# W2's magnitude sums in the weight products, its ternary blocks made on VectorE in tiles 0 to 2 and kept in DRAM

## The chip, the cores and the metric

One Trainium2 chip, all 8 NeuronCores. Each core takes one of the 8 sequences (2048 tokens of 1024 features) and runs the same program alone; nothing is exchanged. The metric is the device time of the slowest core in microseconds. PE is TensorE, ACT is ScalarE, DVE is VectorE, POOL is GpSimd, and SP only issues transfers and waits for what they need; its queue is taken in program order, so a transfer that waits holds back the ones behind it.

## The reference, cut to what matters

Two layers. Layer 0 adds a decayed causal attention and an int4-quantised projection with a low-rank term. Layer 1 adds a chunked linear recurrence (here a masked scores product per tile of tokens) and an FFN whose weights are rounded to -1, 0, 1:

```python
def _quantize(W):
    gamma = jnp.mean(jnp.abs(W))
    return jnp.clip(jnp.round(W / (gamma + EPS)), -1.0, 1.0)
Wq1 = _quantize(W1)                        # W1 is 4096 x 1024
Wq2 = _quantize(W2)                        # W2 is 1024 x 4096
h = jax.nn.relu(jnp.einsum('bsd,fd->bsf', x, Wq1) + b1)
out = jnp.einsum('bsf,df->bsd', h, Wq2) + b2
```

So each matrix (16 MB in f32) is read twice: once for the mean of its magnitudes, once to compare it with plus and minus half of gamma.

## The kernel before, in words

Every engine's program is one list in program order; `do` appends an instruction with the tokens it waits for, and a token is a semaphore count. There is no scheduler: the order of the Python calls is the order on each engine. PSUM is eight banks of 128x512 f32, taken in turn (`take`), and `freed[b]` is the eviction that a bank's next user waits for.

The stages in order: the product Wvo, the first norm and layer 0's V for 16 chunks of 128 tokens; then two weight products of 16 groups of 8 matmuls each, **Wp** (L484 to L493, W_read by W_write) and **G** (L496 to L506, Wq by Wk), each group evicted by ACT. `kern`, the int4 matrix, is loaded behind Wp (L519) and rounded by DVE. Then four tiles of 512 tokens (`j`). Each tile runs `scores0(j)` (P blocks, masked and evicted by DVE), `out0(c)` for its four chunks (P by V and x by Wf, then residual, norm and a transposing DMA), `gproj(j+1)` (8 groups, ACT evicts), `vproj` of four chunks (8 groups, ACT evicts), `scores1(j)` (4j+4 groups, DVE evicts to P) and `pv1(c)` (P by V, DVE adds). The FFN follows: per tile 32 groups `ffn1(j, fc)` with a Relu on ACT, and two `pair(c)` calls, each a Strassen product of 2x2 blocks: seven products of 16 matmuls from differences of h (`diff`, DVE, L1010) and sums of W2 blocks (`w2_sum`, DVE, L981).

The FFN's weights are made beside the tiles. `stat_unit` (L581) sums one 128x1024 block's magnitudes on ACT: 32 blocks of W1, then 32 of W2, each loaded by SP four units ahead, from tile 0's `out0` to tile 2's. `thr_sums` and `thr_scale` turn the sums into thresholds. `w1_begin` and `w1_end` (L810, L815) make a ternary W1 block on DVE in two instructions, in tiles 2 and 3. W2 is made in tile 3 and during `ffn1(0)`: `w2_begin` (L827) takes two signs on ACT, `w2_end` (L835) adds them on DVE, which gives 0 and plus or minus 2, and the Relu has the scale 0.5 for it. `w2_sums` mixes the 20 block sums in between.

SBUF limits when things can be made: W2's ternary blocks lie in R0 and R1, free only after `out0(15)` and `gproj(3)`; W1's in R5 and R2, and R2 holds Wf until `out0(15)`.

Of the kernel before, what the change touches and what calls it, by code (L numbers as in the profile page):

```python
# [14 lines left out]
D = 1024  # L15
# [74 lines left out]
def build_nc():  # L90
# [27 lines left out]
    res_d = nc.dram_tensor("res_d", [T, D], F32, kind="Internal").ap()  # L118
    bnc = nc.dram_tensor("bnc", [1, 16], F32, kind="Internal").ap()
# [156 lines left out]
    ch_yt = [chan(f"yt{k}") for k in range(6)]  # L276
# [206 lines left out]

    Wp = XR.ap().bitcast(BF16)  # L484
    wp_tok = [None] * 16
    for dc in range(8):
        for hf in range(2):
            b = take()
            t_wm = group(b, [(R[3][:, k * 1024 + dc * 128:k * 1024 + (dc + 1) * 128],
                              R[4][:, k * 1024 + hf * 512:k * 1024 + hf * 512 + 512],  # L490
                              t_ww[k // 4], t_wr[k // 4]) for k in range(8)])
            wp_tok[2 * dc + hf] = ev_act_scale(
                Wp[:, dc * 1024 + hf * 512:dc * 1024 + hf * 512 + 512], b, alp, t_wm, t_al, *nrm[12:])  # L493

# [4 lines left out]
    for dc in range(8):  # L499
        for hf in range(2):  # L500
# [5 lines left out]
                G[:, dc * 1024 + hf * 512:dc * 1024 + hf * 512 + 512], b, 1.0 / 32.0, t_gm)  # L506


    kqf = [Rf[3][:, 0:2048], Rf[3][:, 2048:4096], Rf[4][:, 0:2048], Rf[4][:, 2048:4096]]
    ch_kn = [chan(f"kn{k}") for k in range(4)]  # L510
# [6 lines left out]
    t_kn = []  # L517
    for k in range(4):
        t_kn.append(ch_kn[k].dma(sp, kqf[k], rows(kern, 2 * k, 2), t_wm))  # L519
# [45 lines left out]

    ch_st = [chan(f"st{k}") for k in range(4)]
    st_used = [None] * 4
    st_n = [0]
    st_land = [None] * 64

    def stat_load(u):
        k = u % 4
        if u < 32:
            dc, q = divmod(u, 4)
            src = bass.AP(W1T.tensor, 128 * dc * DFF + q * 1024, [[DFF, 128], [1, 1024]])
        else:
            src = rows(W2T, u - 32)
        fr = st_used[k] if u >= 4 else wf_tok[15]
        st_land[u] = ch_st[k].dma(sp, st_slot[k], src, fr)

    def stat_unit(n=1):  # L581

        for _ in range(n):
            u = st_n[0]
            if u >= 64:
                return
            st_n[0] += 1
            k = u % 4
            st_used[k] = act.do(lambda s, k=k, u=u: s.activation(  # L589
                st_slot[k], st_slot[k], AF.Abs, accum_out=wsum[:, u:u + 1]), st_land[u], t_ldb[2])  # L590
            if u + 4 < 64:
                stat_load(u + 4)

    t_thr = [None]
    ch_bt = chan("bt")

    def thr_sums():
        dve.quiet(lambda v: v.reduce_sum(gs[:, 0:1], wsum[:, 0:32], axis=AX.X), st_used[3])
        tb = dve.do(lambda v: v.reduce_sum(gs[:, 1:2], wsum[:, 32:64], axis=AX.X))
        t1 = pool.do(lambda g: g.tensor_reduce(gsr[0:1, :], gs, axis=AX.C, op=ALU.add), tb)  # L600
        t1 = ch_bt.dma(sp, bnc[0:1, 2:4], gsr[0:1, :], t1)
        t_thr[0] = ch_bt.dma(sp, gsr, bass.AP(bnc.tensor, 2, [[0, 128], [1, 2]]), t1)

    def thr_scale():
        t1 = pool.do(lambda g: g.tensor_scalar(gsr, gsr, 1.0 / (DFF * D), EPS_BN, ALU.mult, ALU.add), t_thr[0])
        pool.quiet(lambda g: g.tensor_scalar(thr, gsr, 0.5, None, ALU.mult), t1)
        t_thr[0] = pool.do(lambda g: g.tensor_scalar(nthr, gsr, -0.5, None, ALU.mult))

# [23 lines left out]
    def scores0(j):  # L632
        for i in range(4 * j, NCH):
# [9 lines left out]
                P[:, i * 512:i * 512 + w], pb[b][:, 0:w], mask[m][:, 0:w], ALU.mult), tok, mk_tok[n])  # L643
# [84 lines left out]
    def pv1(c):  # L728
# [11 lines left out]
        ch, q = (ch_ys, pool) if c < 8 else (ch_yt, sp)  # L740
        y_tok[c] = ch[c % 6].dma(q, bass.AP(res_d.tensor, c * 128 * D, [[D, 128], [1, D]]), buf, t)


    xrs = [XR[:, 1024 * k:1024 * k + 1024] for k in range(4)]
    stage = st_slot + xrs + [MC[:, :], b2r[:, :]]
    ch_g = [chan(f"g{k}") for k in range(10)]
    stage_free = [None] * 10

    order = [0, 1, 2, 3] * 8 + [4, 5, 6, 7] * 4 + [9, 8, 0, 1] * 4
    w2_order = [h + 4 * q + i for q in range(4) for h in (0, 16) for i in range(4)]  # L750
    w1_tok = [None] * 4
    w2_tok = [None] * NF
    q_user = [None] * 10
    q_done = {}
    q_tok = {}
# [9 lines left out]
    def unit_load(u):  # L765

        s = order[u]
        if stage_free[s] is None or (q_user[s] is not None and q_user[s] not in q_done):
            return False
        if u < 32:  # L770
            fb, dc = divmod(u, 8)
            src = bass.AP(W1T.tensor, 128 * dc * DFF + fb * 1024, [[DFF, 128], [1, 1024]])
        else:
            src = rows(W2T, w2_order[u - 32])
        q_tok[u] = ch_g[s].dma(sp, stage[s], src, *stage_free[s])
        q_user[s] = u
        return True

    def unit_done(u, t):
        q_done[u] = t  # L780
        stage_free[order[u]] = (t,)

    class Units:


        def __init__(self, lo, hi, begin, end):
            self.ld, self.nx, self.hi = lo, lo, hi
# [415 lines left out]
```

## Time and profile before

| | |
|---|---|
| time, median of 3 runs | 1036.56 us (1035.12 to 1140.85) |
| profiled execution | 1036.97 us, span 1035.4 us |
| spans of the eight cores | 1025.7 to 1035.4 us |
| mean granted TensorE clock of the cores | 0.983 to 0.993 |
| busy: PE, DVE, ACT, POOL | 978.0, 486.0, 382.2, 107.8 us |
| DMA | 133.9 MB, mean 129 GB/s |

A row of a timeline has the start, how long the group lasted from its first start to its last end, the engine, the line, the operation with its tiles and shapes, the count, and in brackets the idle time before it and who ended it. PE's rows can lack a few matmul records. In a table of stretches the columns are the stretch, the busy time of PE, weight loads, DVE, ACT and POOL with the number of instructions, then the granted clock, the DMA engines' share and their rate.

### The profile page before, as it was taken

What the parts mean: (1) busy time and instruction counts of PE and PEld (TensorE: products, weight loads), DVE (VectorE), ACT (ScalarE), POOL (GpSimd) and SP (SyncE); (2) the same over time, 40 slices, a digit from 0 to 9 for tenths busy, and PEclk for the clock granted to TensorE, in tenths of its full rate; (3) what the DMA queues carried; (4) which work ended last, traced back from release to release, by engine and by line L of the source; (5) the groups of instructions that cost most, each with busy time, mean ns of one, the idle gap of its engine ahead of it and who ended that gap; (6) DMA issues with size and microseconds to landing.
All of it is one profiled execution on the core that took longest, in us unless ns stands there. A gap on an engine that the chain in (4) does not pass through costs nothing.

```text
span 1035.4 us, 12956 instructions; the slowest of 8 cores (1025.7 to 1035.4 us)
## 1 busy us (share of the span) xinstructions
PE 978.0 (94%) x4579; PEld 447.4 (43%) x4656; DVE 486.0 (47%) x658; ACT 382.2 (37%) x609; POOL 107.8 (10%) x93
## 2 busy tenths in 40 slices
PE   4899999999999999999896988989999999999998
PEld 1445444444444454445342333434444444444443
DVE  0587025633145144568687789693007300730073
ACT  0566433425865744310125686600330033003300
POOL 3200000045014301600320000000000000000000
PEclk9999999999999999999999899999999999999999
DMA  9999551079897982547358775102100210020001
GB/s 137 198 232 226 94 162 47 1 215 207 244 304 216 259 262 92 124 141 231 104 149 257 240 254 198 41 31 92 41 1 31 91 41 1 31 92 1 1 31 51
DMA packets 58544, 133.91 MB, mean 129 GB/s; under 512 B 21458, under 2 KB 21842, under 8 KB 58482
## 3 DMA queue, kind: packets, MB, share of 16 engines
q1 hardware_dynamic: 48082, 107.76, 34.5%
q0 software_dynamic: 10112, 25.24, 11.6%
q8 instruction: 38, 0.62, 0.2%
q14 instruction: 24, 0.20, 0.1%
q10 hardware_dynamic: 288, 0.10, 0.0%
HBM read 124.75 MB, written 16.78 MB: 137 GB/s over the span
## 4 chain that ended last, share of the span: by engine, by line
PE 80%; DMA 7%; DVE 6%; issue 4%; ACT 2%; POOL 1%; SPq 0%; DVEq 0%; ACTq 0%; POOLq 0%
PE pb L232 69%; PE pb L683 10%; DMA XR<-W2T 2%; DMA R<-WoT 2%; DVE R L989 1%; DVE R L837 1%; DMA b2r<-W2T 1%; DVE R L818 1%; DMA R<-W1T 1%; POOL R L81 1%; PE pb L310 1%; ACT xnat L830 1%; DVE P L721 1%; PE pb L542 0%; DVE xnat L299 0%
## 5 line engine op out<-in xcount | busy, mean ns | idle before, releaser
L232 PE MATMUL pb<-XN,R 128*128 128x512 bf16 x1251 | 278.5, 382 | 11.9 <-ACT V L947 10.3
L232 PEld LDWEIGHTS pb<-XN,R 128*128 128x128 fp8e4 (+1 forms) x1280 | 125.6, 98 | 164.3 <-issue 15.9
L947 ACT ACTIVATE V<-pb,smallS 128x512 bf16<-128x512 f32 x128 | 85.5, 685 | 251.4 <-PE pb L232 251.4
L232 PE MATMUL pb<-R,XN 128*128 128x512 bf16 (+3 forms) x561 | 117.6, 361 | 1.2 <-ACT R L348 0.4
L232 PE MATMUL pb<-R,P 128*128 128x512 fp8e4 x512 | 113.7, 383 | 5.1 <-DVE P L1017 5.1
L1017 DVE TENSOR_TENSOR P<-V 128x2048 bf16<-128x2048 bf16 x32 | 38.1, 1218 | 166.0 <-ACT V L947 166.0
L1046 DVE TENSOR_TENSOR R<-pb,R 128x512 f32<-128x512 f32 x80 | 52.6, 686 | 78.4 <-PE pb L232 78.3
L232 PEld LDWEIGHTS pb<-R,P 128*128 128x128 bf16 x512 | 50.4, 99 | 67.2 <-issue 8.3
L232 PEld LDWEIGHTS pb<-R,XN 128*128 128x128 bf16 x576 | 53.8, 98 | 57.8 <-issue 4.0
L589 ACT ACTIVATE R<-R 128x1024 f32<-128x1024 f32 x64 | 67.1, 1050 | 13.7 <-DMA R<-W1T 8.3
L232 PE MATMUL pb<-R 128*128 128x512 bf16 x314 | 69.2, 379 | 1.1 <-ACT R L343 0.8
L683 PE MATMUL pb<-V,P 128*128 128x512 bf16 x268 | 64.3, 380 | 4.8 <-DVE P L642 4.5
L232 PE MATMUL pb<-V,P 128*128 128x512 bf16 x265 | 61.3, 389 | 7.0 <-DVE P L721 5.3
L232 PE MATMUL pb<-XN 128*128 128x512 bf16 (+3 forms) x316 | 61.3, 353 | 5.1 <-DVE P L721 4.9
L683 PE MATMUL pb<-R,XN 128*128 128x512 bf16 x251 | 61.3, 385 | 0.2
L232 PE MATMUL pb<-XR,V 128*128 128x512 fp8e4 x256 | 56.6, 379 | 0.0
L232 PE MATMUL pb<-XR,XN 128*128 128x512 bf16 x250 | 55.7, 379 | 0.7 <-DMA XN<-xnat 0.4
L232 PEld LDWEIGHTS pb<-R 128*128 128x128 bf16 x320 | 31.2, 98 | 38.5 <-issue 1.2
L702 POOL TENSOR_TENSOR R<-R,b2r 128x1024 f32<-128x1024 f32 x16 | 37.9, 2371 | 92.2 <-ACT R L701 90.1
L232 PEld LDWEIGHTS pb<-XN 128*128 128x128 bf16 x320 | 30.7, 99 | 36.4 <-issue 7.8
L348 ACT CAST V<-pb 128x512 bf16<-128x512 f32 x64 | 35.9, 589 | 25.3 <-PE pb L232 24.9
L691 DVE TENSOR_TENSOR R<-pb,R 128x512 f32<-128x512 f32 x32 | 21.5, 686 | 49.0 <-PE pb L683 37.3
(112 smaller groups left out, 901.9 us busy)
## 6 DMA issues: line engine op xcount, KB each, us to landing
R<-W1T SPq DMA_DIRECT2D x64, 512.0 KB, 6.0
R<-W2T SPq DMA_DIRECT2D x40, 512.0 KB, 5.9
XR<-x SPq DMA_DIRECT2D x16, 512.0 KB, 8.8
R<-x POOLq DMA_DIRECT2D x16, 512.0 KB, 10.4
XR<-W2T SPq DMA_DIRECT2D x16, 512.0 KB, 5.8
R<-res_d SPq DMA_DIRECT2D x16, 512.0 KB, 4.0
out<-R SPq DMA_DIRECT2D x32, 256.0 KB, 2.0
R<-kern SPq DMA_DIRECT2D x4, 1024.0 KB, 12.2
```

The lines of the kernel that those rows point to most:

```text
L81: q.prog.append((after, lambda e: e.dma_start(dst, src, **kw), self.sem, 16))
L232: t.matmul(o, lhs, rhs, start=f, stop=l))
L310: fn = (lambda p, dc=dc: p.transpose(pbB[b][:, dc * 128:(dc + 1) * 128], o[:, dc * 128:(dc + 1) * 128], ident[:, :]))
L348: t = act.do(lambda s: s.copy(o, pb[b][:, 0:n]), tok, *after)
L589: st_used[k] = act.do(lambda s, k=k, u=u: s.activation(st_slot[k], st_slot[k], AF.Abs, accum_out=wsum[:, u:u + 1]), st_land[u], t_ldb[2])
L683: t.matmul(pb[bs[hf]][:, :], lhs, rhs, start=f, stop=l))
L691: t = dve.do(lambda v, hf=hf: v.tensor_tensor(buf[:, hf * 512:hf * 512 + 512], pb[bs[hf]][:, :], buf[:, hf * 512:hf * 512 + 512], ALU.add) ...
L702: b2_tok[c] = pool.do(lambda g: g.tensor_add(buf, buf, b2r[:, :]), tr, t_b2)
L721: t = dve.do(lambda v, b=b, a=a, k=k: v.scalar_tensor_tensor(P[:, a:a + 512], pb[b][:, :], rx[:, -k - 1:-k], CV, ALU.mult, ALU.mult), tok, ...
L947: t = act.do(lambda s: s.activation(hid(fc), pb[b][:, :], AF.Relu, scale=0.5, bias=b1h[:, fc:fc + 1]), tok, t_b1h)
L1017: d_tok[k] = dve.do(lambda v: v.tensor_tensor(dst, Hv[:, x[0], x[1]], Hv[:, y[0], y[1]], ALU.subtract), h_tok[15] if k == "6" else h_tok[3 ...
L1046: done[blk] = dve.do(lambda v, blk=blk, op=op: v.tensor_tensor(r[blk], r[blk] if op == ALU.subtract else pb[b][:, :], pb[b][:, :] if op == ...
```

## The change

1. `stat_unit`'s order is turned round: W2's 32 blocks first, then W1's. Twenty of W2's sums now run during the weight products, six behind the last six groups of Wp and fourteen behind the first fourteen of G, with the P tile as four staging buffers. The other twelve run in `gproj(0)` and `scores0(0)`, W1's thirty-two in tiles 0 to 2, with two staging buffers each.
2. W2's threshold is ready in tile 0. `w2_unit` makes one ternary block by the two DVE instructions that W1 had (`low` and `high`), over the block just read, and SP stores its 128 KB to the DRAM tensor `w2q_d`. Two buffers take turns: the load of a block waits for the store of the one two before it. The 32 units are spread over tiles 0 to 2.
3. In tile 3 `w2_fetch` reads the blocks back: 2 MB and 1 MB before `vproj`, the last 1 MB (into the place of two staging buffers) after the last W1 unit.
4. The 20 sums stand together at the start of `ffn1(0)`. The ACT signs are gone, the Relu has no scale.
5. The stores of chunks 8 to 15 to `res_d` go through POOL's queue, as those of 0 to 7 did. kern's load is issued before G's sums; the small tables come after them.

```diff
+    def stat_place(n):
+        if n < 20:
+            return n % 4, n - 4
+        if n < 32:
+            return 6 + n % 2, n - 2 if n >= 22 else -1
+        return 4 + n % 2, n - 2 if n >= 34 else -1
...
+    for n in range(4):
+        stat_load(n, lgt[15], t_k[1])
     Wp = XR.ap().bitcast(BF16)
...
                 Wp[:, dc * 1024 + hf * 512:dc * 1024 + hf * 512 + 512], b, alp, t_wm, t_al, *nrm[12:])
+            if dc >= 5:
+                stat_unit()
+    for k in range(4):
+        t_kn.append(ch_kn[k].dma(sp, kqf[k], rows(kern, 2 * k, 2), t_wm))
...
                 G[:, dc * 1024 + hf * 512:dc * 1024 + hf * 512 + 512], b, 1.0 / 32.0, t_gm)
+            if dc < 7:
+                stat_unit()
+    for n in range(20, 22):
+        stat_load(n, t_gm)
...
+    def low(a, src, e, tok):
+        return dve.do(lambda v: v.tensor_scalar(
+            A8s[a], src, nthr[:, e:e + 1], None, ALU.is_lt, saturate=False), tok, a_free[a], t_thr[e])
+    def high(a, dst, src, e, tok, *after):
+        a_free[a] = dve.do(lambda v: v.scalar_tensor_tensor(
+            dst, src, thr[:, e:e + 1], A8s[a], ALU.is_gt, ALU.subtract, saturate=False), tok, *after)
+    def w2_load(u):
+        k = u % 2
+        w2_land[u] = ch_w2[k].dma(sp, st_slot[2 + k], rows(W2T, u), w2_kept[u - 2] if u > 1 else st_tok[30 + k])
+    def w2_unit():
...
+        if 0 < u < NF - 1:
+            w2_load(u + 1)
+        src = st_slot[2 + k]
+        dst = src.bitcast(FP8)[:, 0:1024]
+        t = high(k, dst, src, 1, low(k, src, 1, w2_land[u]))
+        w2_kept[u] = ch_w2s[k].dma(sp, w2q_d[:, u * 1024:u * 1024 + 1024], dst, t)
...
     for ec, t_g in gproj(0):
-        pass
+        if ec % 2 == 1:
+            stat_unit()
...
+        if j == 3:
+            w2_fetch(0, 16, t_o0[15], xb_tok[15])
+            w2_fetch(16, 8, t_o0[15])
         for m in range(4):
             t_v1 = vproj(4 * j + m, Wp, wp_tok)
-            stat_unit()
+            if j < 2:
+                if m != 2:
+                    w2_unit()
+                if m % 2 == 1 or j == 1 and m == 0:
+                    stat_unit()
...
             if j == 3:
-                w1u.step(2, t_o0[15])
+                w1_unit(1 + m % 2, t_o0[15])
...
+    w2_fetch(24, 8, w1_done[30], w1_done[31])
...
-            if j == 0 and fc in (0, 2, 4, 6, 9, 11, 13, 15, 18, 20, 22):
-                w2u.step(1)
-                w2_sums(2)
+                for q in range(4):
+                    for n in ("12+22", "21+11", "11-22"):
+                        w2_sum(n, q, t_v1, w1_done[31])
+                    for n in ("11+12", "21+22"):
+                        w2_sum(n, q, s_tok["12+22", q], s_tok["21+11", q])
```

**SP's queue around the weight products.** The rows are SP's transfers in program order, target<-source with the shape; R<-kern is the int4 matrix, MC and A the mask tables. Before:

```order
L81 DMA XR<-x 128x1024 x12
L81 DMA b2r<-b 128x1024
L81 DMA MC<-tabF 128x512 x2
L81 DMA A<-negT 128x512
L81 DMA R<-kern 128x2x1024 x4
L81 DMA R<-tabF 128x1024
L81 DMA R<-negT 128x512
L81 DMA R<-b 128x1024
```

Now:

```order
L81 DMA XR<-x 128x1024 x12
L81 DMA P<-W2T 128x1024 x10
L81 DMA R<-kern 128x2x1024 x4
L81 DMA P<-W2T 128x1024 x10
L81 DMA R<-W2T 128x1024 x2
L81 DMA b2r<-b 128x1024
L81 DMA MC<-tabF 128x512 x2
L81 DMA A<-negT 128x512
L81 DMA R<-tabF 128x1024
L81 DMA R<-negT 128x512
L81 DMA R<-b 128x1024
```

Ten block loads stand ahead of kern and ten behind it, and the tables come last.

**DVE in tile 0, from the end of `out0(3)` to `pv1`.** xnat is the normalised chunk, the evictions to P are `scores1(0)`'s. Before:

```order
L299 TENSOR_SCALAR xnat<-R,col 128x1024
L718 TENSOR_TENSOR P<-pb,MC 128x512
L718 TENSOR_TENSOR P<-pb,MC 128x384
L718 TENSOR_TENSOR P<-pb,MC 128x256
L718 TENSOR_TENSOR P<-pb,MC 128x128
L736 TENSOR_TENSOR R<-pb,R 128x512 x8
```

Now (the two rows of a unit, `low` and `high`, stand seven times in turn where the dots are; two of them are shown):

```order
L299 TENSOR_SCALAR xnat<-R,col 128x1024
L791 TENSOR_SCALAR A<-R,col 128x1024
L795 SCALAR_TENSOR_TENSOR R<-R,col,A 128x1024
L791 TENSOR_SCALAR A8b<-R,col 128x1024
L795 SCALAR_TENSOR_TENSOR R<-R,col,A8b 128x1024
...
L745 TENSOR_TENSOR P<-pb,MC 128x512
L745 TENSOR_TENSOR P<-pb,MC 128x384
L745 TENSOR_TENSOR P<-pb,MC 128x256
L745 TENSOR_TENSOR P<-pb,MC 128x128
L763 TENSOR_TENSOR R<-pb,R 128x512 x6
```

DVE had nothing between the norm and the first P eviction; seven units are there now.

## Rows read from the trace of the kernel before

**Rows 1.** Busy time by stretches; columns as told above.

```profile
560.00:600.00 40.00, 32.85 (x148) 14.64 (x150) 30.97 (x37) 28.72 (x27) 0.00 (x0) 0.91 0.77 254
```

**Rows 2.** PE's timeline from tile 3's scores1 to the first pair.

```profile
530.26 20.88 PE L232 MATMUL pb<-XN 128*128 128x512 bf16 x94
555.70 5.75 PE L232 MATMUL pb<-XN 128*128 128x512 bf16 x24 [4.56 <-DVE P L721]
...
614.91 13.60 PE L232 MATMUL pb<-XN,R 128*128 128x512 bf16 x55 [4.09 <-ACT V L947]
...
665.76 7.07 PE L232 MATMUL pb<-XR,V 128*128 128x512 fp8e4 x32
...
684.98 8.75 PE L232 MATMUL pb<-R,P 128*128 128x512 fp8e4 x32 [4.01 <-DVE P L1017]
```

**Rows 3.** ACT's timeline: evictions of G, gproj(0)'s last, then magnitude sums in tile 0.

```profile
140.95 0.60 ACT L343 ACTIVATE R<-pb 128x512 bf16<-128x512 f32 x1 [1.04 <-PE pb L232]
...
165.13 0.60 ACT L343 ACTIVATE R<-pb 128x512 bf16<-128x512 f32 x1 [1.13 <-PE pb L232]
...
180.66 0.58 ACT L348 CAST R<-pb 128x512 bf16<-128x512 f32 x1 [0.27 <-PE pb L232]
...
229.83 1.04 ACT L589 ACTIVATE R<-R 128x1024 f32<-128x1024 f32 x1
...
230.87 1.04 ACT L589 ACTIVATE R<-R 128x1024 f32<-128x1024 f32 x1
...
259.59 1.06 ACT L589 ACTIVATE R<-R 128x1024 f32<-128x1024 f32 x1
...
261.58 1.07 ACT L589 ACTIVATE R<-R 128x1024 f32<-128x1024 f32 x1
```

**Rows 4.** DVE's groups by shape: busy us, mean ns of one, idle before.

```profile
L989 DVE TENSOR_TENSOR R<-R 128x2048 fp8e4<-128x2048 fp8e4 x12 | 26.8, 2284 | 0.1
...
L818 DVE SCALAR_TENSOR_TENSOR R<-R,col,A 128x1024 fp8e4<-128x1024 f32 x16 | 20.4, 1277 | 0.0
...
L721 DVE SCALAR_TENSOR_TENSOR P<-pb,col,MC 128x512 bf16<-128x512 f32 x24 | 17.7, 746 | 33.7 <-PE pb L232 33.7
...
L812 DVE TENSOR_SCALAR A<-R,col 128x1024 fp8e4<-128x1024 f32 x16 | 12.0, 747 | 10.7 <-DMA R<-W1T 10.3
```

**Rows 5.** The chain of waits: start, us, what; tile 3 and ffn1(0).

```profile
523.52 3.04 DMA XN<-xnat
...
617.45 11.34 DMA b2r<-W2T
```

**Rows 6.** Busy time by stretches of 8 us.

```profile
120.00:128.00 8.00, 7.95 (x38) 3.64 (x38) 0.00 (x0) 3.44 (x5) 0.00 (x0) 1.00 0.00 0
...
620.00:628.00 8.00, 7.95 (x38) 3.64 (x38) 8.00 (x5) 4.96 (x7) 0.00 (x0) 1.00 0.99 371
```

**Rows 7.** Timeline: kern's issues on SP, DVE's first and last reduction of it.

```profile
139.21 3.24 SPq L81 DMA_DIRECT2D R<-kern  x4
...
146.23 2.29 DVE L524 TENSOR_REDUCE col<-R 128x1 f32<-128x2048 f32 x1 [31.06 <-DMA R<-kern]
...
156.29 2.29 DVE L524 TENSOR_REDUCE col<-R 128x1 f32<-128x2048 f32 x1 [0.26 <-DMA R<-kern]
```

**Rows 8.** PE's timeline: gproj(0), gproj(1), and pv1(0)'s start.

```profile
166.59 13.98 PE L232 MATMUL pb<-XN,R 128*128 128x512 bf16 x63
...
250.25 13.76 PE L232 MATMUL pb<-XN,R 128*128 128x512 bf16 x62
...
282.22 4.26 PE L232 MATMUL pb<-V,P 128*128 128x512 bf16 x19
```

**Rows 9.** The answer on the tensor W2T, time to landing.

```profile
DMA to landing us min/median/max: 3.3/5.9/12.1
```

**Rows 10.** The page's DMA issues: KB each, median us to landing.

```profile
out<-R SPq DMA_DIRECT2D x32, 256.0 KB, 2.0
...
res_d<-R SPq DMA_DIRECT2D x8, 512.0 KB, 5.5
```

## What I expect of it

> **What bounds it.** I read the cores and the granted clock first, then TensorE's (PE's) busy time in stretches, its own timeline where it pauses, and last the engines it waits for. All cores are within 1%, and the profiled execution lasted 1036.97 us (span 1035.4), 0.04% over the median, so the sum is made against it. PE is the bound nearly everywhere; in 560 to 600 it is busy 32.9 of 40 us at a mean granted clock of 0.91 [rows 1]. The pauses lie between the start of tile 3's scores1 (530.26) and the fifth product of the first pair (684.98): 4.56 us behind a P eviction, 4.09 behind a Relu, 4.01 behind a diff [rows 2]. The work there is 116 matmuls of scores1 (12 groups of 8, and 20 for the narrow four), 116 of pv1 (2 x (13+14+15+16)), 256 of ffn1, 64 of four products: 552. A group of 8 takes 1.727 us ((165.13 - 140.95)/14 [rows 3]), so the work is 119.2 us; 154.7 pass. **35.5 us are waits and low clock.** What ends them is the making of W2: two signs on ScalarE, an add on DVE, and the sums between, all queued ahead of evictions.
>
> **Term 1, W2's work leaves tile 3: -34.2.** The signs, the adds and their loads go. What stays on DVE during ffn1(0) is 20 sums of 2.28 us [rows 4], 45.7 us. They begin some 4 us into ffn1 (the last W1 unit and two evictions stand before them) and end by 50, under ffn1's 55.3; the third stretch of sums needs the last 1 MB fetch, some 5 us, and is 22 us away. So diffs no longer queue behind sums. The low clock behind the last pause goes too: 32 matmuls took 8.75 us after it and 7.07 before it [rows 2]: 1.7 us. A new wait stays. SP now fetches 3.15 MB of ternary W2 right after the last transposition (523.52 [rows 5]); at 371 GB/s [rows 6] that is 8.5 us, and W1's fifth load queues behind it to about 536. DVE then closes six units before the first scores1 eviction, at about 541; before, it had eight units there. Per pair of groups it needs two evictions and a unit, about 2 x 0.75 + 0.75 + 1.28 = 3.5 us [rows 4] against PE's 3.45, so the lag stays until the last narrow groups, and pv1(12), which begins after 25 us (555), waits for its P block until about 558: +3. Sum: -35.5 - 1.7 + 3 = -34.2. Bounds: +0 (the lag is caught up) and +9 (the loads come 6 us later).
>
> **Term 2, W2's magnitude sums move into the weight products: +14.7.** ScalarE can do it: two evictions and a sum start to start are 1.99 us, a sum alone 1.04 [rows 3], so eviction plus sum is 1.52 against 1.727. The DMA can't. From 120, a few groups into Wp, the queues are empty [rows 6], the first four loads land well before their use at 131, but the next ones start only as sums free their slots. The sixth sum ends at about 141.1 (Wp's last eviction, 139.2, plus 0.69 and 1.04, some queueing), and in SP's order kern's four 1 MB loads come next (issued in 3.24 us [rows 7]), then again ten stat loads. The kern loads land one after the other, 3.15 MB from 146.23 to 156.29, 313 GB/s [rows 7], and a small load behind six others took 11.34 us [rows 5]: the queue is served in order. With 1 MB of stat loads ahead and a start 2 us later the last kern load lands 3.4 us later, at 159.7, and the eleventh stat load behind it at 161.4. That sum is due at 148.9: ScalarE waits 12 us, and every eviction of G behind it. Eight banks hold PE for 13.8 us; the real price comes at the end. The next nine loads land 1.67 us apart (0.52 MB at 313 GB/s), the twentieth sum starts at 176.4, and the fifteenth eviction of G, which every group of gproj(0) needs, ends at 176.4 + 1.04 + 0.5 = 178. It ended at 165.7 [rows 3], and the first group, begun at 166.6 [rows 8], reached its last matmul 1.5 us later, at 168.1. **+10.** The tables for masks, half of which were loaded long before, now stand behind stat loads 20 to 22 (3.3 us) and are 1.8 MB (5.9 us): the masks, ahead of gproj's evictions on ScalarE, come at about 187, as much later as PE. But three more sums stand between gproj's evictions and the last of them, which scores0 waits for as it did at 180.66 [rows 3]: 3 x 1.04, **+3**. A pause of 8 us or more costs the low clock after it, 1.7 as above. Bounds for all of term 2: +3 if the bytes interleave well (12.6 MB from 131 at 371 GB/s end at 165, and then ScalarE's own 1.52 us pace decides), +18 if the tables bring a second pause of 4 us with its clock.
>
> The Trainium skill, page "HBM Reference", section "Specifications (TRN2)", gives a core about 358 GB/s when both of a pair stream. By that, kern would take 11.7 us instead of 13.4 and each load 1.46, term 2 would be near +11, and the whole 1015. A stretch of this trace shows 371, the kern loads 313; the sum keeps 313, for it is the same transfer at the same place.
>
> **Term 3, 32 W2 units on DVE in tiles 0 to 2: +1.** Each is 0.75 + 1.28 us, 65 us in all; DVE was idle over half of the time there, and the ten in out0 sit between chains that PE doesn't wait for. The tight place is a block of seven units from the end of out0(3) to scores1(0), twice (tile 1 has it too). Each of two slots goes load, unit, store, and the next load waits for the store to land: three such cycles, less one store, stand between the issue of the load for the block's third unit (8 us after gproj begins at 250.25 [rows 8]) and the seventh unit's end. A W2T load took 3.3 at least and 5.9 in the middle with four in flight [rows 9]; a 256 KB store 2.0 [rows 10]. I take 4.5 + 1.95 + 2.0 = 8.45, for at most two loads are in flight, and a 128 KB store is nearest to the 256 KB one. The seventh unit ends at 8 + 25.4 - 2 = 31.4, scores1 ends at 32 (282.22 - 250.25), and there pv1 wants its first P, which an eviction after that unit makes: half a microsecond each. Bounds: 0 with 3.3, and 4.5 per block with 5.9, plus its clock.
>
> Small edits at nothing: the bias halving (one 128x32 instruction), the Relu's scale (same instruction), the stores of res_d in tiles 2 and 3 that go from SP's queue to POOL's (POOL has nothing else due, and the reload is wanted only 55 us later). If POOL's store became late, res_load would be, and the pair's first gather with it. The waits at 484 to 526 stay; W1's loads there are the same.
>
> **Sum: 1036.97 - 34.2 + 14.7 + 1 = 1018.5, taken as 1018.** A measurement of this kernel tells about 2% from no change, that is below 1016 or above 1057.
>
> **Rivals.**
> *The weight stage swallows the sums.* If the loads get through between kern's, ScalarE's pace decides: term 2 is +3, the clock stays, the rest as above: 1036.97 - 34.2 + 3 + 1 = 1007. For it: the DMA is idle from 120, and 371 GB/s has been moved. Against: kern's landings one behind the other, and the eleventh load's place behind them. 0.24.
> *The blocks of units are late.* With the 5.9 us load each block ends 4.2 us later: 2 x (4.2 + 1.7) = 12, less the 1: 1029. For: the median load. Against: it belongs to four in flight. 0.17.
> *Slower than before: the round trip through DRAM.* The next load waits for the store of ternary bytes. If a load takes 5.9 and the store 5.5, as the res_d stores of SP did [rows 10], the cycle is 13.35 instead of 8.45, three of them 14.7, less 3.5 for the longer last store: 11.2 us per block, two blocks 22, two more units in tile 1's scores1 5, clock 3.4: 1018 + 30 = 1048. Against: a quarter of the bytes, and an emptier queue. It turns a gain into a loss once the cycle is above 11 us. 0.09. The Trainium skill, "DMA: Bandwidth & Descriptors", section "Anatomy of one DMA — SWDGE (gpsimd) path", told of GpSimd's path, warns of a surprisingly long delay when a completed write has HBM as its target, which speaks for this rival; the 2.0 us stores of out in this trace speak against it.
>
> **Numbers.** The forecast has 0.46, with its own range 1011 to 1026; the three rivals 0.24, 0.17 and 0.09, and 0.04 is for what I don't see. Eight in ten reaches from the quick case with term 1 at its best (1004) to the late blocks with their bounds: 1003 to 1034. Faster by over 2%: the quick case, and of the forecast's own range the third below 1016: 0.24 + 0.15 + 0.01 = 0.40. Slower by over 2% needs the DRAM cycle at its worst or something unseen: 0.05. Within: 0.55.
>
> **What would show it.** ScalarE's timeline between 140 and 180: one wait of about 12 us for a W2T load, and PE idle some 10 us before gproj(0) (right); no such wait (the quick rival). DVE's first scores1 eviction in tiles 0 and 1 within a microsecond of PE's, or several behind. In tile 3 no pause over 4 us, ffn1(0) in 55 us from first to last group, and the sums done before it ends. If PE still pauses in ffn1(0), term 1 is wrong; if pv1(12) waits for much more than 3 us, the fetch is the cause.

## The result and the profile after

The changed kernel takes **1063.51 us** (median of 4 runs, 1061.57 to 1065.93) against 1036.56 for the kernel before, run beside it: ratio **1.0258** (1.0223 to 1.0294), slower. Forecast were 1018 us and a range that ended at 1034. Executions in which one die ran at a lower clock (1140.85 us, say, for the kernel before) are left out of every ratio; two of e9_early_late's four were such, so it has none and stands again, unchanged, as e12_early_late.

Where it goes is read first from the starts of the program's stages on PE. Each number below is the start of a stage's first matmul, as the median over the eight cores of a kernel's profiled execution, minus the same of the kernel before. The three columns are the three terms of the prediction: term 2 is the shift at gproj(1), term 3 what comes on top until tile 3's scores1, term 1 what comes after, until ffn1(1) starts (behind all that tile 3's W2 work had delayed). The last column is the time against the kernel before on the same chip, with its 95% interval; less than 2% either way counts as the same time.

| kernel | term 2 (to gproj(1)) | term 3 (to scores1(3)) | term 1 (to ffn1(1)) | ratio |
|---|---|---|---|---|
| predicted | +14.7 | +1 | -34.2 | 0.982 |
| changed kernel | +18.2 | **+34.9** | -27.7 | 1.0258 |
| e1_a8 | +20.4 | +28.3 | -26.8 | 1.0250 (1.0233-1.0267) |
| e2_weights | +21.6 | +33.7 | -27.3 | 1.0262 (1.0238-1.0286) |
| e3_fetch_late | +21.4 | +35.5 | **-35.7** | 1.0184 (1.0139-1.0229) |
| e4_all | +22.0 | +27.4 | -35.7 | 1.0132 (1.0112-1.0151) |
| e5_noload | +16.8 | **+3.2** | -25.7 | 0.9917 (0.9903-0.9932) |
| e6_nogloads | +11.3 | +32.9 | -28.5 | 1.0170 (1.0150-1.0190) |
| e7_early | +17.2 | **+8.5** | -27.8 | 1.0011 (0.9993-1.0028) |
| e8_aside | +19.4 | +20.8 | -27.8 | 1.0187 (1.0159-1.0215) |
| e9_early_late | +19.3 | +9.0 | -35.2 | (as e12) |
| e10_room | **+0.3** | +44.5 | -35.6 | 1.0086 (1.0054-1.0119) |
| e11_spread | +1.2 | +35.4 | -35.9 | 1.0047 (1.0028-1.0065) |
| e12_early_late | +18.9 | +10.1 | -35.7 | **0.9942 (0.9920-0.9964)** |
| e13_trip | +0.4 | +29.5 | -35.6 | 0.9992 (0.9965-1.0018) |
| e14_now1sums | +0.6 | +13.9 | -35.5 | 0.9774 (0.9759-0.9790) |
| e15_last | +0.3 | +32.4 | -35.8 | 0.9988 (0.9972-1.0004) |

The lines below are the changed kernel's slowest core (span 1061.0). **Tile 3**, PE's timeline (start, us, instruction, in brackets the idle time before it and what ended it), which answers [rows 2]:

```profile
583.92 13.98 PE L233 MATMUL pb<-XN 128*128 128x512 bf16 x64
600.00 11.41 PE L233 MATMUL pb<-XN 128*128 128x512 bf16 x64 [2.10 <-DVE P L748]
612.70 2.32 PE L233 MATMUL pb<-V,P 128*128 128x512 bf16 x10 [1.29 <-DVE P L748]
...
618.99 24.29 PE L233 MATMUL pb<-V,P 128*128 128x512 bf16 x104 [2.08 <-DVE P L745]
643.12 55.42 PE L233 MATMUL pb<-XN,R 128*128 128x512 bf16 x256
698.37 7.07 PE L233 MATMUL pb<-XR,V 128*128 128x512 fp8e4 x32
705.27 13.98 PE L233 MATMUL pb<-R,P 128*128 128x512 fp8e4 x64
```

All 256 matmuls of ffn1(0) are one line of 55.42 us and the products follow at full pace: the pauses of before are gone. From scores1(3) to ffn1(0) 59.2 us pass for 50.1 of work, so new waits of 9 us are left; DVE's and SP's timelines name the cause:

```profile
592.43 0.75 DVE L791 TENSOR_SCALAR A8b<-R,col 128x1024 fp8e4<-128x1024 f32 x1 [7.48 <-DMA R<-W1T]
```
```profile
578.56 0.95 SPq L81 DMA_DIRECT2D R<-w2q_d  x2
579.60 32.69 SPq L81 DMA_DIRECT2D R<-W1T  x10
```

W1's next load stands behind the 3 MB fetch, and DVE's evictions stand behind the block that waits for it.

**Weight stage and tile 0**, first ScalarE's timeline, then DVE's, then two lines of DVE's before (answers to [rows 3, 7]):

```profile
161.88 1.06 ACT L519 ACTIVATE P<-P 128x1024 f32<-128x1024 f32 x1 [13.16 <-DMA P<-W2T]
...
191.71 0.81 ACT L653 ACTIVATE R<-R 128x128 f32<-128x128 f32 x2 [11.88 <-DVE R L650]
```
```profile
150.94 2.29 DVE L594 TENSOR_REDUCE col<-R 128x1 f32<-128x2048 f32 x1 [35.50 <-DMA R<-kern]
...
160.32 2.29 DVE L594 TENSOR_REDUCE col<-R 128x1 f32<-128x2048 f32 x1 [0.46 <-DMA R<-kern]
162.72 0.16 DVE L596 TENSOR_REDUCE col<-col 128x1 f32<-128x4 f32 x1
174.79 0.15 DVE L601 TENSOR_SCALAR col<-col 128x1 f32<-128x1 f32 x1 [11.92 <-DMA col<-bnc]
...
191.26 0.75 DVE L650 SCALAR_TENSOR_TENSOR R<-R,col 128x128 f32<-128x128 f32 x2 [5.49 <-DMA R<-negT]
```
```profile
164.85 0.15 DVE L531 TENSOR_SCALAR col<-col 128x1 f32<-128x1 f32 x1 [6.01 <-DMA col<-bnc]
...
175.75 0.74 DVE L624 SCALAR_TENSOR_TENSOR R<-R,col 128x128 f32<-128x128 f32 x2
```

Kern's last block is 4.0 us later than before (160.32 against 156.29); forecast was 3.4. Behind it stands a chain: the maximum goes through DRAM to all partitions (11.92 us between; before 6.01), the quantisation, and the first mask, which now waits 5.49 us for its table. 4.0 + 5.9 + 5.5 = 15.4: the first mask comes at 191.26 where it came at 175.75. ScalarE's exponential of it (191.71, after a wait of 11.88) stands in front of gproj(0)'s evictions, and PE has eight banks. But PE's own gproj(0), held by G's evictions behind the wait of 13.16, ends only at 193.85: in this kernel the two paths end together.

**The units.** DVE's timeline in tile 0's scores1 block, then SP's at its start:

```profile
281.30 0.75 DVE L791 TENSOR_SCALAR A8b<-R,col 128x1024 fp8e4<-128x1024 f32 x1 [3.58 <-DMA R<-W2T]
282.16 1.29 DVE L795 SCALAR_TENSOR_TENSOR R<-R,col,A8b 128x1024 fp8e4<-128x1024 f32 x1
285.58 0.75 DVE L791 TENSOR_SCALAR A<-R,col 128x1024 fp8e4<-128x1024 f32 x1 [2.14 <-DMA R<-W2T]
...
290.90 0.75 DVE L791 TENSOR_SCALAR A8b<-R,col 128x1024 fp8e4<-128x1024 f32 x1 [3.18 <-DMA R<-W2T]
...
295.93 0.75 DVE L791 TENSOR_SCALAR A<-R,col 128x1024 fp8e4<-128x1024 f32 x1 [2.88 <-DMA R<-W2T]
...
300.40 0.75 DVE L791 TENSOR_SCALAR A8b<-R,col 128x1024 fp8e4<-128x1024 f32 x1 [2.33 <-DMA R<-W2T]
...
304.48 0.75 DVE L791 TENSOR_SCALAR A<-R,col 128x1024 fp8e4<-128x1024 f32 x1 [1.94 <-DMA R<-W2T]
...
306.54 1.68 DVE L745 TENSOR_TENSOR P<-pb,MC 128x512 bf16<-128x512 f32 x4
```
```profile
283.52 0.33 SPq L81 DMA_DIRECT2D w2q_d<-R  x1
283.94 0.39 SPq L81 DMA_DIRECT2D R<-W1T  x1
286.08 0.33 SPq L81 DMA_DIRECT2D R<-W2T  x1
```

Every unit waits for its load, and scores1(0)'s evictions, on whose P pv1 waits, come last. A slot comes round after 9.6 us here (281.30, 290.90, 300.40); the forecast had 8.45. In tile 1 a slot takes 13 to 17 us, and behind the units stand the products with the masks:

```profile
327.69 0.75 DVE L791 TENSOR_SCALAR A8b<-R,col 128x1024 fp8e4<-128x1024 f32 x1 [4.12 <-DMA R<-W2T]
...
335.85 0.75 DVE L791 TENSOR_SCALAR A<-R,col 128x1024 fp8e4<-128x1024 f32 x1 [3.62 <-DMA R<-W2T]
```

Between 306 and 345 a W2T load takes 6.9 us in the middle and a 128 KB store 4.5, with x's loads (9.9) and res_d's stores (8.7) among them. Over the program such a store takes 1.7 to 8.6 us, 3.6 in the middle; I had put 2.0.

### The profile page after: what moved, and what is told of

Same layout as the page of the kernel before. It is cut to its first block, busy times and chain, and to the rows that moved or that the text cites. A ratio compares the mean times of both kernels' runs of the same rounds, so it can differ in the third digit from the quotient of the medians.

```text
span 1061.0 us, 13017 instructions; the slowest of 8 cores (1046.2 to 1061.0 us)
## 1 busy us (share of the span) xinstructions
PE 989.5 (93%) x4656; PEld 449.3 (42%) x4656; DVE 512.5 (48%) x689; ACT 313.7 (30%) x545; POOL 118.3 (11%) x105
## 3 DMA queue, kind: packets, MB, share of 16 engines
q1 hardware_dynamic: 52116, 111.95, 34.2%
## 4 chain that ended last, share of the span: by engine, by line
PE 66%; DMA 20%; DVE 7%; issue 3%; ACT 1%; SPq 1%; POOL 1%; DVEq 0%; ACTq 0%; POOLq 0%
PE pb L233 56%; PE pb L710 10%; DMA R<-W2T 6%; DMA w2q_d<-R 4%; DMA P<-W2T 2%; DVE R L795 2%; DMA XR<-x 2%; DMA R<-WoT 2%; DMA R<-negT 1%; DMA R<-W1T 1%; DVE A L791 1%; DMA P<-Wd 1%; DVE xnat L299 1%; SPq L81 1%; ACT P L519 1%
## 5 line engine op out<-in xcount | busy, mean ns | idle before, releaser
L969 ACT ACTIVATE V<-pb,smallS 128x512 bf16<-128x512 f32 x128 | 88.0, 687 | 337.4 <-PE pb L233 337.4
L233 PE MATMUL pb<-R,XN 128*128 128x512 bf16 (+3 forms) x576 | 120.9, 365 | 5.8 <-ACT R L348 5.8
L1068 DVE TENSOR_TENSOR R<-pb,R 128x512 f32<-128x512 f32 x80 | 52.7, 687 | 85.4 <-PE pb L233 85.4
L233 PE MATMUL pb<-V,P 128*128 128x512 bf16 x272 | 67.6, 410 | 16.1 <-DVE P L748 9.6
L710 PE MATMUL pb<-V,P 128*128 128x512 bf16 x272 | 65.5, 381 | 15.1 <-DVE P L668 14.9
L233 PEld LDWEIGHTS pb<-R,P 128*128 128x128 bf16 x512 | 50.1, 98 | 60.4
L710 PE MATMUL pb<-R,XN 128*128 128x512 bf16 x256 | 65.1, 400 | 0.0
L519 ACT ACTIVATE R<-R 128x1024 f32<-128x1024 f32 x44 | 46.2, 1051 | 48.8 <-DMA R<-W1T 46.7
L729 POOL TENSOR_TENSOR R<-R,b2r 128x1024 f32<-128x1024 f32 x16 | 42.7, 2671 | 106.2 <-ACT R L728 106.2
L233 PEld LDWEIGHTS pb<-V,P 128*128 128x128 bf16 x272 | 28.0, 104 | 54.3 <-issue 27.7
L710 PEld LDWEIGHTS pb<-V,P 128*128 128x128 bf16 x272 | 26.7, 98 | 49.6 <-issue 18.9
L791 DVE TENSOR_SCALAR A<-R,col 128x1024 fp8e4<-128x1024 f32 x32 | 26.0, 814 | 38.6 <-DMA R<-W2T 28.9
## 6 DMA issues: line engine op xcount, KB each, us to landing
R<-x POOLq DMA_DIRECT2D x16, 512.0 KB, 10.1
```

The lines of the kernel that those rows point to most:

```text
L233: t.matmul(o, lhs, rhs, start=f, stop=l))
L519: st_tok[u] = act.do(lambda s, u=u: s.activation(slot, slot, AF.Abs, accum_out=wsum[:, u:u + 1]), st_land[u], t_ldb[2])
L710: t.matmul(pb[bs[hf]][:, :], lhs, rhs, start=f, stop=l))
L729: b2_tok[c] = pool.do(lambda g: g.tensor_add(buf, buf, b2r[:, :]), tr, t_b2)
L791: return dve.do(lambda v: v.tensor_scalar(A8s[a], src, nthr[:, e:e + 1], None, ALU.is_lt, saturate=False), tok, a_free[a], t_thr[e])
L969: t = act.do(lambda s: s.activation(hid(fc), pb[b][:, :], AF.Relu, bias=small[:, S_B1 + fc:S_B1 + fc + 1]), tok)
```

## The experiments

**Batch 1: one repair for each term, then all three.** e1_a8 takes the store out of the units' ring:

```diff
-        dst = src.bitcast(FP8)[:, 0:1024]
+        dst = A8s[k]
-        w2_kept[u] = ch_w2s[k].dma(sp, w2q_d[...], dst, t)
+        w2_made[u] = t
+        w2_kept[u] = a_free[k] = ch_w2s[k].dma(sp, w2q_d[...], dst, t)
     # the load of unit u waits for w2_made[u - 2], not for w2_kept[u - 2]
```

> The changed kernel, but high writes the ternary block over the low mask in A8 or A8b and the store reads from there, so the next W2T load waits only for VectorE, not for the store to land. Theory 1 (round trip: load, unit, store in one slot set the pace of the units, and VectorE's evictions stand behind them): the 32 us that PE lost between gproj(1) and out0(8) go almost wholly, the two-slot cycle falls from 10 us and more to about 7, and the span from 1061 to 1030 to 1036. Theory 2 (65 us of added VectorE work is too much beside the evictions): at most 5 us go, 1056 or more. Theory 3 (the added DMA traffic makes each load slow): the loads stay as late as they are, about half comes back, 1045 or more.

Measured: 28.3 instead of 34.9 us of term 3, and no gain in time (the slowest core decides, and term 2 was 2 us worse). The wait for the store was real, but it was 6.6 us of the price. DVE still waits for 18 of the loads:

```profile
DVE A L792 <- DMA R<-W2T: 28.6, 9, 6.5
DVE A8b L792 <- DMA R<-W2T: 24.0, 9, 6.8
```

(the answer on waits between 190 and 600: us in total, times, longest; the changed kernel has 28.9 and 26.0). SP's order shows a cause: the load of unit u+1 stands behind one of W1's sum loads, which waits for ScalarE:

```profile
322.78 0.33 SPq L81 DMA_DIRECT2D w2q_d<-A  x1
325.19 0.33 SPq L81 DMA_DIRECT2D R<-W1T  x1
325.57 0.79 SPq L81 DMA_DIRECT2D R<-W2T  x1
```

e2_weights moves sums and tables in the weight stage (ten in Wp's product, four in G's, six in gproj(0), twelve in scores0(0); b2, MS, CV and ngm loaded ahead of all).

> The changed kernel with the sums placed otherwise: ten behind Wp's last ten groups, four behind G's first four, six in gproj(0), twelve in scores0(0); and b2, MC and A8's tables loaded before all of them, as in the kernel before. Theory 1 (the sums' loads wait behind kern's 4 MB, and the tables behind both): the 21 us lost up to out0(0) fall to 3 or less, span 1041 to 1045. Theory 2 (ScalarE cannot hold eviction plus sum): the pauses stay, now also in Wp, 1058 or more.

Measured: +21.6, no gain. ScalarE's wait of 13.16 us is gone (4.6 are left, in seven pieces), but kern is issued at 147.54, its last block is reduced at 166.93 (changed kernel 160.32), and the first mask comes at 192.03, no sooner than 191.26. PE is done with gproj(0) at 183.55 and then waits 10.35 us for an eviction behind that mask: here the chain behind kern alone decides, though this run made kern later too. e3_fetch_late puts `w2_fetch(0, 16)` and `w2_fetch(16, 8)` behind the scores1(3) loop.

> The changed kernel with the first two fetches of the ternary W2 (3 MB) issued after scores1(3)'s last unit, not before vproj. Theory 1 (W1's fifth load waits behind the fetch, VectorE 7.5 us for it, pv1 pays): from scores1(3)'s start to ffn1's 59.2 us become 51 to 53, span about 1054, a ratio to before near 1.018. Theory 2 (VectorE's load of two evictions and a unit per pair of groups sets it): 57 or more, no change of the time. A later fetch could also hold up the block sums: then ffn1(0) is longer than 55.3 us.

Measured: as expected. Term 1 goes from -27.7 to -35.7, and in every later kernel with this edit it is -35.2 to -35.9. e4_all has the three edits.

> The three edits together. If the three losses are independent (32, 21 and 6 us of the 1061), the span is 1002 to 1008, 3% under the kernel before. If one only hides another (the units late in tile 0 because the weight stage is late, say), it stays above 1015.

Measured: 27.4 us of term 3 and all of term 2 stay. The first repair took some of its loss, the second none; only the third hit its cause in full.

**Batch 2: which part of a unit costs?** e5_noload and e8_aside start from e1_a8 and leave the units' loads out, or send them elsewhere; e7_early moves one line; e6_nogloads thins the weight stage.

```diff
 # e5_noload
-        w2_land[u] = ch_w2[k].dma(sp, st_slot[2 + k], rows(W2T, u), ...)
+        w2_land[u] = w2_land[u - 2] if u > 1 else ch_w2[k].dma(...)
 # e7_early, in w2_unit()
-        if 0 < u < NF - 1:
-            w2_load(u + 1)
         ...
         w2_kept[u] = a_free[k] = ch_w2s[k].dma(...)
+        if u + 2 < NF:
+            w2_load(u + 2)
 # e6_nogloads
-        st_land[n] = ch_st[k].dma(...)
+        st_land[n] = st_tok[n - 4] if 10 <= n < 20 else ch_st[k].dma(...)
```

> The kernel of run e1_a8, with the 30 loads of W2's rows for the units 2 to 31 left out (the units work on the blocks of the units 0 and 1, so W2's ternary matrix is not W2's here); VectorE's two operations, the store and everything else stay. Theory A (VectorE waits for a 512 KB load that was issued only one unit ahead, with the evictions and masks of the tile queued behind it): the waits DVE <-DMA R<-W2T (some 50 us in the tiles) vanish, and with them most of what tiles 0 to 2 lost behind the gate product of tile 1: of the 32.7 us (medians over the cores: from gproj(1) at +18 to gproj(4) at +45, with +51 at gproj(3)) at least 24 come back; time about 1032 to 1042 us. Theory B (VectorE's own 2 us a unit, put in front of evictions that TensorE needs, are the cost): the loss stays, over 1055 us. Between the two each part shows its size.

> As e5_noload, but each of the 30 loads is still made, of the same rows and bytes at the same place in SP's queue, into a spare DRAM tensor that nobody reads (W2's ternary matrix is again not W2's): the traffic without VectorE's wait. If the wait for the load alone costs (theory A), as fast as e5_noload within 5 us. If it is the bytes (theory C: the queues are full in the tiles, and the extra 16 MB a core make the sums', the residual's and the other loads late), it stays where e1_a8 was, 1060 to 1070 us.

> The kernel of run e1_a8, with the load of unit u+2 issued right behind unit u's store (that is as soon as VectorE has made unit u) instead of at the start of unit u+1, so that two loads are under way most of the time. Everything is computed. Theory A: the load gains about one unit's distance (8 to 10 us) on landings of 5 to 10 us, so most of the waits go: 20 or more of the 32.7 us, time 1036 to 1048 us. If landing times grow as more is under way (theory C), less than 8 us: over 1055 us.

> The changed kernel with the loads of the sums 10 to 19 left out (ScalarE sums old blocks in their place, at the same time in its order; W2's threshold is not W2's here): ScalarE's work in the weight products without this traffic behind kern. Theory K (what the weight stage and tile 0 lose comes of kern's loads, 4 MB issued at 139 us, landing late behind and beside the sums' loads, then the scale's round trip through DRAM, the quantisation, the masks and the evictions of gproj(0) one behind the other): scores0(0) starts near 184 instead of 194 us (before: 180), gproj(1) at +6 or less instead of +18, time 1050 to 1054 us. If ScalarE's sums themselves hold up the evictions (theory S), it stays over 1060 us.

e5_noload: term 3 falls from 28.3 to **3.2** us with all 64 DVE operations and all stores in place. DVE's own work is nearly free; the loads are the price. e7_early computes everything, and its term 3 is **8.5**: the same loads and bytes, issued ahead of the sum's load. This is SP's timeline there, and the waits between 286 and 470:

```profile
308.96 0.33 SPq L81 DMA_DIRECT2D w2q_d<-A8b  x1
309.33 0.44 SPq L81 DMA_DIRECT2D R<-W2T  x1
309.87 0.49 SPq L81 DMA_DIRECT2D R<-W1T  x1
```
```profile
DVE A L792 <- DMA R<-W2T: 12.8, 7, 3.5
...
DVE A8b L792 <- DMA R<-W2T: 7.2, 6, 1.7
```

20 us of waits, where e1_a8 has 53 in the same stretch. The one line is worth 20 of the 28 us of term 3 and 2.4% of the time (ratio 1.0250 to 1.0011).

The line moves a whole unit's place in the Python text, and I had expected a unit's length from it. SP's queue says otherwise: in both kernels a load waits for the same unit and stands between the same two stores; only what stands ahead of it there differs. On e1_a8's slowest core, of 30 such loads 20 were behind sums' loads, issued 31.7 us in all after the store before them, and DVE waited 42 us for these 20; eight were behind the transposing transfers of out0, issued 76 us late in all, and cost DVE 7.5. In e7_early every load follows its store by 0.4 us. Whether the 1.6 us a load, or the 512 KB no longer ahead of it in the queue, did more is not separated. (The Trainium skill, page "DMA: Bandwidth & Descriptors", section "Rules for kernel authors", advises to issue a transfer early and wait for it late; the changed kernel waits late but issues late too.)

e8_aside doesn't decide: some cores are as fast as e5_noload (1031.5), others as slow as e1_a8 (1059.3). The transfers to a spare tensor share SP's queue, so DVE now waited for the store of its buffer (31.4 + 15.4 us on the slowest core). Its term 3 of 20.8 us shows that the loads' bytes, sent elsewhere, can still cost much in another form.

e6_nogloads: scores0(0) starts at 182.8 (changed kernel 193.8, before 180.2): theory K holds to that point. But gproj(1) is still 11.3 us late, 5 more than expected, and the time 1056.39 a little over the 1050 to 1054 expected. The first mask comes 6.0 us later than before (medians over the cores; 13.8 in the changed kernel); the rest is lost among gproj(0)'s evictions, with sums between them, some of which wait for their load (1.22 and 0.83 us on the slowest core).

**Batch 3: repairs together.** e9_early_late is e7_early with the late fetch; e12_early_late is the same kernel again.

> The kernel of run e7_early (ternary block made in A8s[k], next load right behind the store) and, as in e3_fetch_late, the fetches of W2's blocks 0 to 23 behind scores1(3). Everything is computed. If the fetch of 3 MB delays W1's blocks in tile 3 here as it did in the changed kernel (e3 against the changed kernel: gproj(3) to ffn1(0) 156.7 against 165.2 us, medians over the cores), the same 8 us come off: 1030 to 1035 us, ratio to before 0.992 to 0.996. If with punctual units tile 3 has slack enough, nothing: 1040 us as e7_early.

> The same kernel as e9_early_late, once more, since only part of its executions there could be compared: 1030 to 1035 us if W1's blocks of tile 3 stood behind the fetch, 1040 us if not.

Measured: **ratio 0.9942** (1029.72 to 1034.03 us), as expected: 3% faster than the changed kernel, and 0.6% under the one before, which the interval keeps apart from 1 but which is within the 2% that counts as the same. In tile 3 nothing is left to wait for; PE's timeline (50.4 us from scores1 to ffn1, work 50.1):

```profile
561.85 25.23 PE L233 MATMUL pb<-XN 128*128 128x512 bf16 x128
586.91 25.48 PE L233 MATMUL pb<-V,P 128*128 128x512 bf16 x116
612.23 55.42 PE L233 MATMUL pb<-XN,R 128*128 128x512 bf16 x256
```

e10_room empties the queue in front of kern: four sums in Wp's product, kern issued next, four loads behind it, tables, then sums 8 to 31 in tile 0, the units ten places later.

> Everything is computed. e9_early_late and in the weight stage: tables first; only W2's sums 0 to 3 (loaded before) during Wp's product; kern's loads issued at the end of that product with nothing of the sums ahead of them; sums 4 to 7 loaded behind kern and taken in the last evictions of G's product; sums 8 to 31 in tile 0 (scores0(0), out0(0), gproj(1)), two to four loads ahead; the units and W1's sums moved back by about ten places. Theory K (kern's late landing and the chain behind it cost most of the 18 us up to gproj(1)): scores0(0) starts at 181 to 184 us (changed kernel 194, before 180), gproj(1) at +3 to +7 instead of +17, and if the tiles keep what e9_early_late has, the time is 1018 to 1026 us. The rival (theory T: tile 0 and 1 have no room on ScalarE for the moved sums, which stand in front of evictions and masks there): what the weight stage gives back is lost again by gproj(2), over 1030 us.

Theory K holds: term 2 is **+0.3**. The run moves kern, the tables and gproj(0)'s sums together, so it prices them as one. DVE's timeline of the chain (the changed kernel's is above):

```profile
158.34 2.29 DVE L598 TENSOR_REDUCE col<-R 128x1 f32<-128x2048 f32 x1 [1.67 <-DMA R<-kern]
160.73 0.16 DVE L600 TENSOR_REDUCE col<-col 128x1 f32<-128x4 f32 x1
166.91 0.15 DVE L605 TENSOR_SCALAR col<-col 128x1 f32<-128x1 f32 x1 [6.03 <-DMA col<-bnc]
...
177.81 0.74 DVE L654 SCALAR_TENSOR_TENSOR R<-R,col 128x128 f32<-128x128 f32 x2
```

Yet the rival's time came out: gproj(2) was 16 us late again, ratio 1.0086 (1046.32 to 1051.44 us). Its cause did not: with 24 sums in tile 0, scores0(1) still began only 0.3 us late, and the 16 us were lost behind that. In scores0(1) the units stood 3 to 5 us apart and DVE waited 8.29 us for one load.

**Batch 4: why do the tiles take it back?** e11_spread makes more sums early and spreads the units; e13_trip moves the threshold's two small transfers from SP's queue to POOL's (and two units by one place); e14_now1sums is e13_trip without 28 loads of W1's sums; e15_last issues W1's first four loads sooner.

> Everything is computed. e10_room with the W2 sums done earlier and the units spread wider: sums 0 to 3 and 4 to 7 during Wp's product (all loaded before kern), 8 to 11 loaded behind kern and taken at the end of G's product, 12 to 31 in tile 0 (three in each out0(0..3), as many as the kernel before had there), so that the threshold is known at gproj(1) and not at scores1(0); three units in vproj(0), only three (not five) in scores0(1), the last in vproj(2). If e10_room lost its 16 us in tile 1 and its 8 in tile 2 and 10 in scores1(2) to units that stood closer than their loads of 9 us could follow, and to W1's late threshold, then gproj(2) starts at 337 to 342 us (e10_room 352, before 336), gproj(3) at 428 to 433 (453, 423) and the time is 1012 to 1022 us. If only the sum of the transfers counts, wherever the units stand, tile 1 still loses 10 or more: over 1030 us.

> Everything is computed. e11_spread with the threshold's two small transfers on POOL's queue and no longer in SP's order, the loads of the first two units thereby ahead of them (in e11_spread they stood behind: the sum was ready at 259.6 us, the first unit ran at 275.9, VectorE waiting 16.2 us), the first unit one place later and one more in scores0(2). If this trip and SP's order cost tile 0 and the start of tile 1 their 7 us (scores1(0) at +3.4, scores0(1) at +7.5 against before), scores0(1) starts at 286 to 288 us (e11_spread 293.6) and the time falls by 5 to 8 us, to 1035 to 1039. If the tiles hand back whatever comes early, because what bounds them is the sum of transfers up to gproj(3), it stays at 1041 to 1045.

> e13_trip with the loads of W1's sums from the fifth on left out (28 loads of 512 KB; ScalarE sums old blocks in their place, W1's threshold is not W1's here): the units, their loads and stores stay where they are. If the tiles 1 and 2 of these kernels are bound by the sum of the transfers (14 MB less here), or the units' loads are late because W1's loads share the queue, gproj(3) comes at 424 to 430 us (e11_spread 447.7, before 422.6) and the time is 1010 to 1022. If it is VectorE's own work of 2 us a unit in front of its evictions, less than 6 us come back.

> Everything is computed. e13_trip with its last W2 unit in gproj(3) instead of vproj(2), and W1's first four loads issued at the end of gproj(3) again, as in the changed kernel (in e13_trip they were issued at 478.0 us behind that unit's store, W1's first block waited 4.9 us at 482.35, and scores1(2) to scores0(3) took 42.5 us against 36.3 in e12_early_late, medians over the cores). If those late loads were the 6 us, 1029 to 1033 us, ratio to before 0.990 to 0.994; if tile 2 is at its limit of transfers, 1036 to 1039.

e11_spread: gproj(2) at 353.0, as e10_room; spreading alone gained 9 us later on. SP's order cost some of it, as e13_trip shows: scores0(1) starts at 287.0 instead of 293.6, and the ratio falls from 1.0047 to 0.9992, some 6 us. In e11_spread the sum was ready at 259.56, and (DVE's timeline)

```profile
259.56 0.19 DVE L533 TENSOR_REDUCE col<-smallS 128x1 f32<-128x32 f32 x1 [2.48 <-ACT R L521]
275.89 0.75 DVE L796 TENSOR_SCALAR A<-R,col 128x1024 fp8e4<-128x1024 f32 x1 [16.15 <-DMA R<-W2T]
```

But e13_trip still loses 29.5 us where e12_early_late loses 10.1: the 18.5 us won in the weight stage are all spent again by scores1(3). e14_now1sums takes 14.7 MB out and term 3 falls to 13.9, the time to 1015.47. Windows of e13_trip, then of e14_now1sums (PE, PEld, DVE, ACT, POOL busy, clock, share of the queues, GB/s):

```profile
260.00:340.00 80.00, 70.26 (x333) 32.11 (x332) 37.44 (x56) 34.34 (x63) 10.96 (x17) 0.91 0.70 222
340.00:420.00 80.00, 77.51 (x383) 36.44 (x380) 56.19 (x72) 31.37 (x57) 20.77 (x13) 1.00 0.84 259
```
```profile
260.00:340.00 80.00, 78.87 (x390) 37.21 (x388) 46.51 (x72) 38.27 (x72) 19.12 (x19) 1.00 0.56 169
340.00:420.00 80.00, 79.25 (x392) 37.44 (x391) 61.77 (x82) 32.76 (x59) 17.02 (x12) 1.00 0.58 175
```

So half of that loss comes of W1's sums' loads beside the units: their bytes, or their places and waits in SP's queue, which this run takes out as well. e15_last gained nothing (its rival, "tile 2 is at its limit of transfers", fits the time, but no run shows such a limit). Open is what the rest is, the bytes, SP's order or the two slots: the kernel before moved 258 GB/s in 320 to 360 and lost nothing (PE busy 39.79 of 40 us), with four loads under way. A third slot for the units wasn't tried.

## Why the prediction was wrong

**Term 3 is the step that failed** (+1 forecast, +34.9 measured, which alone is more than the 27 us of the result). Its sum was "4.5 + 1.95 + 2.0 = 8.45", charged only for two blocks of seven units, in half-microseconds. Three things were wrong in it. First the size: the cycle was 9.6 us in the quiet place and 13 to 17 in tile 1. Then the place: "the ten in out0 sit between chains that PE doesn't wait for" and the units in scores0 were costed at nothing, but each stands in DVE's order before evictions, and 19 units waited 51 us between 286 and 470. Last the cause: I took the store as the doubtful part and the load as given. e1_a8 took the store out of the ring and kept 28.3; e5_noload took the loads out and kept 3.2. What decided was where the load stood in SP's queue, behind a sum's load that waits for ScalarE: e7_early put it ahead and kept 8.5. I had followed DVE's order, not SP's. The third rival (1048, at 0.09) had the effect right, a cycle above 11 us, and its 30 us nearly the size, but named the store, which was worth 6.6: its nearness is luck. (The Trainium skill's warning of a long delay with HBM as the write's target, page "DMA: Bandwidth & Descriptors", section "Anatomy of one DMA — SWDGE (gpsimd) path", is borne out in part: 3.6 us in the middle and up to 8.6 for 128 KB, where out's 256 KB took 2.0 [rows 10]. Both write to DRAM from SP's queue, so the target alone doesn't make the difference; w2q_d's stores ran among loads.)

**Term 2** was near in size (+14.7, measured +18.2, just past its bounds of +3 to +18), and its first half happened as told: ScalarE's wait was forecast as 12 us and was 13.16, kern's last block 3.4 us late and was 4.0. But e2_weights removed that wait and gained nothing. The masks, which I had put "as much later as PE", are a second path of the same length: their chain has the trip through DRAM, which took 5.9 us longer among the loads and for which I had no term. That the forecast by the first path alone came near was in part luck. The rival that the weight stage swallows the sums had against it what I said; with kern first in the queue (e10_room) it does swallow eight of them, at +0.3.

**Term 1** is right in kind: ffn1(0) in 55.4 us, no pause over 4 us. The residue was 9 us instead of 3, its own upper bound and the cause named for it (the fetch ahead of W1's load); without it the gain is 35.7, of 37.2 forecast.

The sum of the errors: 3.5 + 33.9 + 6.5 = 43.9, against 1063.51 - 1018 = 45.5.

## What to carry to other kernels

When work moves to another engine, write down the order of the queue that feeds it, not only of the engine: what stands before each load, and what that waits for. Read it from the queue's timeline, since a call's place in the program text does not tell it. Here one line that puts each load ahead of another stream's was worth 2.4%. And a transfer with a long chain behind it (kern, then its scale) goes ahead of the megabytes of prefetch: term 2 was 18.2 us with sums' loads ahead of kern and the tables last, and 0.3 with both mended and gproj(0)'s sums moved. But ask what the time freed upstream will be spent on before counting it, since here 18 us won at the start were lost again in the tiles.

## What the runs showed of the hardware

- A load's time depends on its company. The same 512 KB W2T load took 4.7 us in the middle over 250 to 600, and 6.9 between 306 and 345; the 512-byte broadcast of one value took 2.8 us in e10_room and 6.0 among the loads of the changed kernel.
- POOL can hold DVE up. In e10_room, DVE's timeline and POOL's:

```profile
450.00 4.82 DVE L299 TENSOR_SCALAR xnat<-R,col 128x1024 bf16<-128x1024 f32 x1
```
```profile
449.60 4.66 POOL L692 TENSOR_TENSOR R<-R 128x1024 f32<-128x1024 f32 x2
```

  The same operation takes 0.80 us elsewhere. It ends with POOL's (454.8 and 454.3). The kernel before has it too (4.44 at 414.61), so no difference here rests on it. The Trainium skill, page "SBUF — State Buffer", section "Who interferes with whom", says that `tensor_scalar` can run in a mode that takes a pair of ports which both engines share, and that the later one then blocks; the trace agrees, for POOL began 0.4 us sooner.
- Pauses cost clock: in 160 to 200 the changed kernel's PE was busy 24.67 us of 40 at a mean granted clock of 0.83, the kernel before 39.36 at 1.00.
